# An early table load, weight preparation moved within VectorE's queue, two more PSUM banks for the first group, and new places for the steps of a hand-ordered kernel

## The reference

```python
x = x + L0_conv(ln_c(x))      # u @ W_in -> values, B, C, dt; dt = softplus(dt + bias); KV = B^T (V * dt * A) per image
                              # y = C @ KV + V * D; layer norm of y; y @ W_out
t = t + L0_ffn(ln_t(t))       # gate: softmax, top 2 of 8; 8 experts 64 -> 128 -> 64 with GELU, weighted and summed
x = x + L1_conv(ln_c(x))      # x / sqrt(3x3 sum of squares per channel + mix of squares over 8 channels + beta)
t = t + L1_ffn(ln_t(t))       # gate: top 2, softmax; 8 experts 64 -> 256 -> 64 with GELU
```

## Time and profile before

| | us |
|---|---|
| median of 3 runs | 538.91 (538.27 to 539.37) |
| the profiled execution | 538.86 |
| its span, first to last instruction | 537.0 |
| PE busy | 459.8 |
| DVE busy | 409.3 |
| ACT busy | 364.3 |
| POOL busy | 258.9 |

### The profile page before, as it was taken

How to read it: one execution, slowest core, us unless ns; L and a number is a source line. 1 busy time by engine, 2 the same in 40 slices (tenths; PEclk the granted TensorE clock), 3 DMA queues, 4 the chain that set the end, 5 groups by cost and what they waited for, 6 DMA issues and landing times.

```text
span 537.0 us, 12527 instructions
## 1 busy us (share of the span) xinstructions
PE 459.8 (86%) x4978; PEld 238.2 (44%) x4978; DVE 409.3 (76%) x832; ACT 364.3 (68%) x446; POOL 258.9 (48%) x217
## 2 busy tenths in 40 slices
PE   0364876864799999999999999999999989999995
PEld 0253344434455545543555355545553444344442
DVE  6536867898899889988998899788987666475422
ACT  2213634834679976987698968896879686777761
POOL 3122163385258166825783478236743470634224
PEclk9999995995799999999999999999999999999998
DMA  6000520520076018500860075007600760150161
GB/s 259 0 21 2 125 56 0 132 50 1 19 184 140 1 40 190 114 1 5 213 143 2 4 199 139 3 2 181 158 2 1 180 159 1 44 139 0 31 141 49
DMA packets 17305, 42.03 MB, mean 78 GB/s; under 512 B 2656, under 2 KB 7904, under 8 KB 17120
## 3 DMA queue, kind: packets, MB, share of 16 engines
q1 hardware_dynamic: 16608, 39.13, 30.4%
q0 software_dynamic: 640, 2.10, 1.3%
HBM read 38.60 MB, written 2.62 MB: 77 GB/s over the span
## 4 chain that ended last, share of the span: by engine, by line
PE 65%; DVE 12%; ACT 10%; issue 7%; POOL 5%; DMA 1%; POOLq 0%; DVEq 0%; ACTq 0%
PE hP L838 25%; PE yP L857 23%; PE sA L692 8%; PE sC L692 4%; ACT H L678 4%; ACT L567 2%; POOL ACC L545 2%; DVE YW L1191 1%; PE sA L699 1%; ACT L678 1%; PE sA L749 1%; POOL stat_b L487 1%; PE sC L796 1%; DVE nacc L1147 1%; ACT proj L600 1%
## 5 line engine op out<-in xcount | busy, mean ns | idle before, releaser
L678 ACT ACTIVATE H<-hP,K 128x1024 f32<-128x1024 f32 x192 | 209.8, 1115 | 48.7 <-PE hP L838 47.4
L838 PE MATMUL hP<-xT,w 128*64 128x512 f16 x1536 | 202.8, 387 | 5.1 <-ACT H L678 4.9
L857 PE MATMUL yP<-H,w 128*64 128x512 f32 x768 | 197.4, 595 | 2.4 <-DVE YW L1191 2.4
L545 POOL TENSOR_TENSOR ACC<-ACC,YW 128x512 f32<-128x512 f32 x96 | 135.4, 1424 | 86.5 <-DVE YW L1191 86.5
L838 PEld LDWEIGHTS hP<-xT,w 128*64 128x64 f16 x1536 | 84.2, 112 | 119.5 <-issue 65.7
L1191 DVE SCALAR_TENSOR_TENSOR YW<-yP,K,WB 128x512 f32<-128x512 f32 x96 | 70.5, 744 | 28.1 <-PE yP L857 23.9
L857 PEld LDWEIGHTS yP<-H,w 128*64 128x64 f32 x768 | 50.7, 137 | 30.2 <-issue 7.8
L1147 DVE SCALAR_TENSOR_TENSOR nacc<-PAD,K,nacc 128x528 f32<-128x528 f32 x56 | 55.8, 997 | 1.4
L484 POOL TENSOR_SCALAR stat_c<-stat_c 128x8 f32<-128x8 f32 x8 | 1.6, 197 | 103.4 <-DVE stat_c L954 103.4
L567 ACT ACT_TABLE_LOAD x22 | 28.2, 1283 | 7.0 <-DVE nacc L1147 4.3
L692 PEld LDWEIGHTS sC<-fold,ACC 128*64 128x64 f32 x512 | 20.8, 143 | 21.2 <-issue 18.5
(11 more groups left out here) (141 smaller groups left out, 617.8 us busy)
## 6 DMA issues: line engine op xcount, KB each, us to landing
WB<-w_scratch SPq DMA_DIRECT2D x128, 256.0 KB, 5.6
X<-in_x SPq DMA_DIRECT2D x8, 256.0 KB, 7.0
out<-X POOLq DMA_DIRECT2D x8, 256.0 KB, 3.9
WB<-in_m_W SPq DMA_DIRECT2D x1, 1024.0 KB, 8.2
WB<-in_m_W SPq DMA_DIRECT2D x1, 512.0 KB, 5.4
w<-in_m_W SPq DMA_DIRECT2D x1, 512.0 KB, 8.9
w_scratch<-wTs SPq DMA_DIRECT2D x16, 32.0 KB, 1.8
K<-in_consts SPq DMA_DIRECT2D x1, 453.5 KB, 6.0
```

Source lines behind the costliest of these rows:

```text
L545: pool.tensor_tensor(ACC[ACC_OF[m]][:, cols], ACC[ACC_OF[m]][:, cols], YW[:, u % 4, :], ALU.add).then_inc(summed, 1)
L678: nc.scalar.activation(H[:, s % RING, :], hP[s % 2][:, :], ACT.Gelu, bias=b1[l][:, e * ch + c:e * ch + c + 1], scale=1.0 / WS)\
L838: mm = nc.tensor.matmul(hP[s % 2][b * C:(b + 1) * C, hf * HALF:(hf + 1) * HALF], w1[l][:, sp, w, b * C:(b + 1) * C], xT[l][g % 2][:, hf * ...
L857: mm = nc.tensor.matmul(yP[hf][a * C:(a + 1) * C, :], w2[l][:, (2 * j + a) * ch + c, :], H[:, (2 * ch * j + 2 * c + a) % RING, hf * HALF:( ...
```

## The change

1. ACT loads the table set EXP_LN as its first instruction, ahead of the wait for the constants, and `tables` starts with it.
2. "out" is prepared right after "experts0", at `norm_a` of group 0; "experts1" after the mixer's split of group 0.
3. For group 0 alone, proj1 and y1 go to yP[0], proj2 and mix_out to yP[1]; these steps don't wait for sA, and drop out of the order of its users.
4. All tables have new places, and the stages new starts (`AB_LEAD`, `AB_SHIFT`, `CD_SHIFT`, `CD_LEAD`).

```diff
 PE_AT = dict(
-    ab=dict(turn_a=1, proj0=4.5, proj1=12, proj2=13, state=17.5, mixer=18.5, y0=19.5, y1=20.5, y_sums=22,
-            mix_out=24, turn_b=32, gate=35.5, send=39.5),
-    cd=dict(turn_c=14.5, pool0=15.5, turn_u=22.5, turn_d=27.5, gate=29, send=32.5),
-    final=(13.5, 14.5, 21.5, 23))
+    ab=dict(turn_a=4, proj0=6.5, proj1=8, proj2=8.5, state=20.5, mixer=22.5, y0=23.5, y1=24.5, y_sums=25.5,
+           mix_out=27, turn_b=34.5, gate=38, send=43),
+    cd=dict(turn_c=13, pool0=15, turn_u=23, turn_d=28, gate=29, send=34),
+    final=(14.5, 15.5, 22.5, 26))
 ACT_AT = dict(
-    ab=dict(sums_a=-19.5, turn_a=3, proj0=3.5, proj1=12, proj2=12.5, decay=13.5, y0=19, y1=19.5, sums_b=26,
-            turn_b=31.5, top2=37.5, send=39.5),
-    cd=dict(sums_c=5, turn_c=13.5, norms=20.5, sums_d=23.5, turn_d=27.5, top2=30.5, send=32.5),
+    ab=dict(sums_a=-15.5, turn_a=5, proj0=6, proj1=8, proj2=8.5, decay=11.5, y0=23, y1=23.5, sums_b=27.5, turn_b=34,
+           top2=40.5, send=42),
+    cd=dict(sums_c=8, turn_c=12.5, norms=21, sums_d=24, turn_d=27.5, top2=29.5, send=34),
 DVE_AT = dict(
-    ab=dict(centre_a=-20, sums_a=-18, norm_a=-6, decay=12.5, values=14.5, state=17.5, mixer=18.5, y_sums=22.5,
-            mix_out=24.5, centre_b=24.5, sums_b=26.5, norm_b=30, top2=34.5, weights=38.5),
-    cd=dict(centre_c=5, sums_c=11, norm_c=13, pool0=15.5, pool1=17.5, pool2=17.5, pool3=19.5, turn_u=22.5,
-            centre_d=22.5, sums_d=24, norm_d=26, top2=30, weights=30),
-    final=(13.5, 14, 21, 25))
+    ab=dict(centre_a=-16.5, sums_a=-7, norm_a=-5.5, decay=11, values=18, state=19.5, mixer=22.5, y_sums=26,
+           mix_out=27.5, centre_b=28, sums_b=29.5, norm_b=34, top2=40, weights=41.5),
+    cd=dict(centre_c=6.5, sums_c=9, norm_c=11, pool0=15, pool1=17, pool2=19.5, pool3=20, turn_u=24, centre_d=24,
+           sums_d=25, norm_d=26.5, top2=30, weights=32),
+    final=(15, 16, 23, 27))
 POOL_AT = dict(
-    ab=dict(sums_a=-17, norm_a=-7.5, state=17.5, y_sums=24, sums_b=30),
-    cd=dict(sums_c=5.5, norm_c=10, scale=21.5, sums_d=26),
+    ab=dict(sums_a=-7.5, norm_a=-5.5, state=24, y_sums=25, sums_b=32.5),
+    cd=dict(sums_c=9.5, norm_c=18, scale=19.5, sums_d=25.5),
 SP_AT = dict(
-    ab=dict(decay=-9.5, send=20),
-    cd=dict(send=23.5, piece1=34, piece2=38, piece3=28),
+    ab=dict(decay=-12.5, send=30.5),
+    cd=dict(send=38.5, piece1=48, piece2=39.5, piece3=41),
-STORE_AT = 45
-AB_LEAD = 38.5
+STORE_AT = 29.5
+AB_LEAD = 40.5
...
-AB_SHIFT = (-0.5, 0, 0, 0, 0, 0, 0, 0)
-CD_SHIFT = (0, 0, 0, 0, 0, 0, -0.5, -2)
-CD_LEAD = 1
+AB_SHIFT = (-1.5, -1.5, -0.5, 0, 0, 0, 0, 0)
+CD_SHIFT = (0, 0, 0, 0, 0, 0, 0, -4)
+CD_LEAD = 1.5
...
+        def a_bank(k, g):
+            return {"proj1": yP[0], "proj2": yP[1], "y1": yP[0], "mix_out": yP[1]}.get(k, sA) if g == 0 else sA
...
-             lambda g, k: a_order.append((k, g)), lambda g, k: c_order.append((C_USES[k], g)), PE_AT)
+             lambda g, k: a_order.append((k, g)) if a_bank(k, g) is sA else None, lambda g, k: c_order.append((C_USES[k], g)), PE_AT)
...
         def _(act):
+            act.preload_act_table_set(EXP_LN)
             act.wait_ge(loaded["first"], 16)
...
-            tables = [None]
+            tables = [EXP_LN]
...
                 elif k in ("proj0", "proj1", "proj2"):
                     n = int(k[-1])
-                    pe.wait_ge(*a_read(k, g))
+                    if a_bank(k, g) is sA:
+                        pe.wait_ge(*a_read(k, g))
...
                         prepare("in")
                         prepare("experts0")
+                        prepare("out")
                 elif k == "decay":
                     dve.wait_ge(pjS.sem, pjS.at(g))
-                    if g == 0:
-                        prepare("out")
...
                     v.tensor_tensor(lo, sA[:, :], hi, ALU.subtract).then_inc(gmixS.sem, 1)
+                    if g == 0:
+                        prepare("experts1")
...
                 elif k == "weights":
                     gate_weights(0, g)
-                    if g == 0:
-                        prepare("experts1")
```

More of the change, by code:

```diff
@@ L600, in ab @@
                     nc.scalar.activation(proj[:, tiles, 0:PROJ],
-                                         sA[:, 0:cols].rearrange("p (t n) -> p t n", n=PROJ), ACT.Copy,
+                                         a_bank(k, g)[:, 0:cols].rearrange("p (t n) -> p t n", n=PROJ), ACT.Copy,
                                          scale=1.0 / WS).then_inc(pjS.sem, 1)
@@ L612, in ab @@
                     act.wait_ge(ymm.sem, ymm.at(g, hf + 1))
-                    nc.scalar.activation(ysq[:, cols], sA[:, :], ACT.Square).then_inc(yev.sem, 1)
-                    nc.scalar.activation(yT[:, cols], sA[:, :], ACT.Copy).then_inc(yev.sem, 1)
+                    nc.scalar.activation(ysq[:, cols], a_bank(k, g)[:, :], ACT.Square).then_inc(yev.sem, 1)
+                    nc.scalar.activation(yT[:, cols], a_bank(k, g)[:, :], ACT.Copy).then_inc(yev.sem, 1)
                 elif k == "sums_b":
@@ L735, in ab @@
                         for s in range(2):
-                            mm = product(sA[:, (t - 3 * n) * PROJ:(t - 3 * n + 1) * PROJ],
+                            mm = product(a_bank(k, g)[:, (t - 3 * n) * PROJ:(t - 3 * n + 1) * PROJ],
                                          xTa[:, t * P:(t + 1) * P], win[:, s, :],
@@ L764, in ab @@
                         for s in range(2):
-                            mm = product(sA[:, (m % 2) * PIX:(m % 2 + 1) * PIX], G2[:, s, m, :],
+                            mm = product(a_bank(k, g)[:, (m % 2) * PIX:(m % 2 + 1) * PIX], G2[:, s, m, :],
                                          xTa[:, m * PIX:(m + 1) * PIX], start=(s == 0), stop=(s == 1))
@@ L774, in ab @@
                 elif k == "mix_out":
-                    pe.wait_ge(*a_read(k, g))
+                    if a_bank(k, g) is sA:
+                        pe.wait_ge(*a_read(k, g))
                     for t in range(T):
-                        mm = product(sA[:, t * C:(t + 1) * C], yT[:, t * P:(t + 1) * P], wout_g[:, :])
+                        mm = product(a_bank(k, g)[:, t * C:(t + 1) * C], yT[:, t * P:(t + 1) * P], wout_g[:, :])
                     mm.then_inc(omm.sem, 1)
@@ L1100, in ab @@
                     dve.wait_ge(yrs.sem, yrs.at(g))
-                    v.tensor_tensor(X1[g % 2][:, :, :], sA[:, :].rearrange("p (t c) -> p t c", t=T),
+                    v.tensor_tensor(X1[g % 2][:, :, :], a_bank(k, g)[:, :].rearrange("p (t c) -> p t c", t=T),
                                     per_tile(stat["n"][:, 3, :], C), ALU.mult).then_inc(x1s.sem, 1)
```

## The result

The changed kernel took 530.61 us, the median of four runs (528.95 to 531.87), against 539.0 us for the kernel before in the same set: ratio 0.9845, 95% interval 0.9817 to 0.9873. Faster by 1.55%, 8.4 us; forecast were 529.9 us and 1.7%. The profiled execution took 529.8 us with a span of 528.0. Here and in the experiments the ratios leave out single executions that took 955 us or more (one each of e2, e11 and e13, and two of the kernel before), the medians do not.

What follows compares the result with a forecast made beforehand. Middle groups were taken as PE-bound (54.3 of 55.25 us busy), so time could be won in the fill and a little in the drain: 538.86 - 8.0 - 1 = 529.9 us, range 524.4 to 534.5.

Steps and rivals of the forecast that it cites:

- Part 1: Group 0 up to its mixer: table load 1.3, prepare("out") 1.9 and bank waits 1.3 go, less 0.6: 3.9 us gained.
- my +0.6: Cost at group 0's decay: VectorE reaches group 1's centring later, and ScalarE's square of group 1 precedes Exp; 0.6 us.
- Part 2: Group 0 from y0 to X1: waits of y1 (1.18) and mix_out (0.26) go, 1.4 us; experts1 costs nothing.
- Part 3: Group 0 from X1 to the first experts: gate 4.5 us earlier, copy of the gate weights 6.4 us earlier.
- Part 4: experts1 out of group 1's chain: first scaling 6.3 us earlier, taken as broadcast-bound; group 1's X1 7 us earlier.
- Part 5: Groups 1 and 2: 1.2 us more at group 1's GELU, 0.7 lost at norm_b, 0.5 to 1 gained at group 2.
- The fill: Everything before the steady conveyor of groups: 7 + 1.2 - 0.7 + 0.5 = 8.0 us gained, bounds 5.3 and 10.5.
- Part 6: The conveyor, the steady middle groups: same instructions in other places, taken as 0, from -3 to +4 us.
- Part 7: The drain: last cd stage starts earlier, gate comes before the last expert run; -1 us (+1 to -2).
- only the head start counts: Rival, 0.17: groups 1 and 2 are held elsewhere, only part 2's 5.3 us arrive and the drain gives nothing: 533.5 us.
- VectorE holds the conveyor: Rival, 0.07: later top2 makes the send late and holds up PE in the middle groups; slower, 541.3 us.
- The clock: Rival, 0.14: denser work in the fill keeps PE's granted clock up, worth 4.4 us more: 525.5 us.

Runs made afterwards that it cites:

- e2: The kernel before's code with the changed kernel's tables of slots, leads and shifts; 542.23 us, ratio 1.0046 to the kernel before.
- e11: e7 with VectorE's norm_c of group 1 moved behind group 3's values and PE's turn_c of group 1 behind group 3's state; 537.34 us.
- e13: Changed kernel plus 154 pairs of unread matmuls ahead of PE's waits, in the first 50 us and for groups 1 and 2; 527.27 us.
- e3: Changed kernel without the early load of the exp/ln table set; 530.57 us, ratio 0.985 to the kernel before.
- e5: Changed kernel with group 0's five mixer parts back in the one bank sA; 534.36 us, ratio 0.9899 to the kernel before.
- e1: The changed kernel's code with the kernel before's tables of slots, leads and shifts; 535.69 us, ratio 0.9943 to the kernel before.
- e4: Changed kernel with experts1's preparation back behind group 0's gate weights; 534.78 us, ratio 0.9925 to the kernel before.
- e7: Changed kernel with group 2's gate weights first on VectorE and group 0's second-layer transpose behind group 2's fourth expert product; 534.11 us.
- e10: Changed kernel plus 45 pairs of unread matmuls ahead of PE's waits in the first 50 us; 527.61 us, ratio 0.9775 to the kernel before.
- e9: Changed kernel plus 18 pairs of unread matmuls ahead of PE's waits, groups 1 and 2 only; 530.96 us, ratio 0.9829 to the kernel before.

## Why the prediction was right

The total came out within 0.7 us of the forecast, and the mechanism of group 0's head is as written. But parts 4 and 5 were too small, and what was lost behind them nearly made up for it; that the sum fits so well is in part luck.

**Part 1** (3.9 us): 4.33 at line 1074 (22.36 to 18.03). The square of group 1 cost almost nothing: it starts at 16.64, VectorE's second small result ends at 17.00 and Exp starts at 17.17, 0.15 us later than it could, so my +0.6 was wrong. Table (1.22 in e3) and banks (1.18 at line 1074 in e5, of its 2.67) came at their rows' price. What they leave of the 4.33 is 1.93, the 1.9 of prepare("out"), which has no run of its own.

**Part 2** (1.4): 1.42, 1.19 at y_sums and 0.23 at the output product, where GpSimd's power is next (VectorE waits 1.86 us for it, which I hadn't named). Sum at X1 5.75, foretold 5.3. experts1 did hide, with 1.56 us to spare instead of 0.7, but only because the tables also put GpSimd's power first (e1).

**Part 3** (gate 4.5, copy 6.4): 5.0 and 6.8, the surplus of part 1.

**Part 4** is the mis-sized term. The first scaling could not come before 58.4, I wrote, and took 7.8 us for the broadcast of the weights; it came at 57.07. The distance from copy to scaling is 6.9 us in the changed kernel, in e3 and in e5. What I took for the broadcast is VectorE's queue. In the kernel before, the scaling starts in the same step as the line ahead of it ends, the mixer's split of group 1:

```profile
64.11 0.69 DVE L1090 TENSOR_TENSOR G<-sA,G 128x512 f16<-128x512 f32 x1
```

It is the same in the changed kernel (56.46 and 57.07), in e2 and in e4. The broadcast ends a wait only two scalings later, at 60.62. And I priced experts1 by its work, 3.7 us, with 6.3 to 8.5 for this group; X1 of group 1 came 9.4 us earlier (64.75; 74.19 before). e4 shows the missing part: a late value stops PE, and after that stop its products took nearly twice their time, 1.74 us on top.

**Part 5**: group 1's first GELU was to come 8.2 us earlier (7 + 1.2) and came 11.1 earlier. Then the error went the other way: group 2 was to keep all but 0.2 of it, and 1.9 was lost. I had seen that VectorE does both gates one after the other, and put no price on what stands behind them; which chain of VectorE's takes the 1.9 us is not settled (e7, e11). The fill came out at 8.5 us, by group 2's first scaling, against 8.0.

**Part 6** (0): the wait for wgt fell to 0.3 us instead of staying, but the waits for GELU rose from 1.7 to 4.7, so PE stands still 1.07 us in a group where it was 0.91. That a group is 0.2 us shorter all the same stands in the windows as busy time of PE (53.99 instead of 54.34); why that is shorter is not shown. 1.75 us were won in three groups, 1.1 of them between the scalings of groups 2 and 3. **Part 7** (-1): +1.3 from group 5 on, the last two groups of the conveyor and the drain together. Again two terms that cancel, both inside their ranges. The upper end of my range is a slip: 538.86 - 5.3 + 0.5 is 534.1, not 534.5.

Of the rivals, *only the head start counts* fails at X1 of group 1, and *VectorE holds the conveyor* at the wait for wgt. *The clock* did not come true for this change: the low stretches only moved (70 to 90 us and 110 to 133 us, granted clock 0.50 to 0.75). But its price was about right: filling PE's waits brought 3.6 us up to the gate weights and some 4 at the end. By the Trainium skill (TensorE: Matmul & The Clock Gate, What's actually happening) the low rate is where the engine rests and activity lifts it; the traces of e10 and e13 agree; in e9 the row stays at 0.50 from 115 to 130 us in spite of the 9 pairs added between 120 and 130.

## What to carry to other kernels

A step moved into an engine's idle time is free only if the queues of the other engines are moved along: code and order were -3.1 and +2.5 us alone, and -8.4 together. Price a delay ahead of an in-order TensorE by the stop and by what the products behind it then take. In a fill with much waiting, products that nobody reads are worth trying: they gave some 4 us here, where three further orders of the steps all lost.

## What the runs showed of the hardware that was not expected

The granted clock of the windows can't be taken at its word in the first 50 us of these traces: it reads 1.00 in the changed kernel while every product takes nearly twice its later time (0.97 us against 0.58 for 12 matmuls of a projection, 1.98 against 1.04 for the mixer's). The durations are the better reading. In e10, whose PE is busier, the row does move; windows of its head (PE, PEld, DVE, ACT and POOL busy, PEclk, DMA, GB/s):

```profile
0.00:10.00 10.00, 4.48 (x20) 1.61 (x20) 5.83 (x19) 2.12 (x3) 3.27 (x12) 1.00 0.74 260
10.00:15.00 5.00, 3.36 (x44) 2.54 (x46) 4.83 (x13) 1.46 (x2) 1.15 (x1) 0.57 0.42 175
15.00:20.00 5.00, 3.64 (x34) 1.95 (x30) 4.39 (x11) 2.08 (x6) 1.78 (x2) 0.75 0.00 0
20.00:25.00 5.00, 3.02 (x44) 1.85 (x46) 3.42 (x10) 0.00 (x0) 2.47 (x3) 1.00 0.02 6
```

The moment at which PE reaches the full rate is not the same in each execution. e9 is the changed kernel's own code up to 69 us, and agrees with it within 0.03 us up to the transpose of group 0's gate weights (49.88 and 49.86); then

```profile
50.20 1.92 PE L859 MATMUL hP<-xT,w 128*64 128x512 f16 x8
52.05 1.08 PE L766 MATMUL sA<-Vs,proj 128*32 128x128 f32 x16
```

stand where the changed kernel has 1.05 and 0.65 us, and KVs comes at 53.72 instead of 52.68. One microsecond of difference between two runs of the same instructions, at one place. The profiled execution of e3 has the like, 1.7 us, between 89 and 97 us.

VectorE's operations can take longer while GpSimd works. In the kernel before, Vs (L1072) takes 1.22 us in four groups and 2.33 in the four where GpSimd's accumulation (L545) runs beside all of it; in the changed kernel it takes 1.22 in all eight. The pooling's nacc (L1147, L1155) takes 0.77 us wherever GpSimd is idle. It takes 1.27 to 1.67, always beside GpSimd, in 18 of 56 cases before and in 3 of 56 after. Working at the same time isn't enough for it: three of the short Vs overlap an accumulation for 0.9 us. Vs, nacc and xnrm together lose 22.6 us of busy time by the new places, and others gain (the decay's second small operation, L1067, 6.0 us instead of 1.8), which leaves the 11.7 us. This is read from two traces; no run tests it, and what it is worth in time is open.
